# The crossed attentions of a two-layer block on one core: another order on all engines

## The reference, cut to what matters

```python
x = x + L0_xattn(layernorm(x), ctx, ...)
x = x + L0_ffn(layernorm(x), ...)            # routed experts and two shared ones
c = layernorm(x)                             # 2048 tokens
char2sub = softmax((c@Wq_c+bq_c) @ (ctx@Wk_s+bk_s).T / 16) @ (ctx@Wv_s+bv_s)
sub2char = softmax((ctx@Wq_s+bq_s) @ (c@Wk_c+bk_c).T / 16) @ (c@Wv_c+bv_c)
sub2char = interp_linear(sub2char, 2048)     # 1601 rows stretched to 2048
gate = sigmoid(concat(char2sub, sub2char) @ Wg + bg)
x = x + gate*char2sub + (1-gate)*sub2char
h = layernorm(x)
p = softmax(h @ gate_W.T);  cnt = sum(p > 0.3)
x = x + (experts 0 and 1 of h, each scaled by its count and its p) @ out_W.T
```

## Time and profile before

| | us |
|---|---|
| median of 3 runs | 1100.87 (1098.93 to 1103.83) |
| the profiled execution's own time | 1102.15 |
| its span, first to last instruction | 1100.3 |
| PE busy (share of the span) | 967.1 (88%) |
| DVE, ACT, POOL busy | 735.5, 588.6, 392.6 |
| mean granted clock of PE | 0.948 |

### The profile page before, as it was taken

The page is one execution under the profiler, slowest core; times in us unless marked ns, Lnnn a source line. Parts: engine busy times, 40 slices in busy tenths (PEclk is TensorE's granted clock), DMA queues, the critical chain, the costliest instruction groups (busy, mean ns, idle before and its releaser), DMA issues.

```text
span 1100.3 us, 19396 instructions
## 1 busy us (share of the span) xinstructions
PE 967.1 (88%) x6934; PEld 907.7 (82%) x6934; DVE 735.5 (67%) x1704; ACT 588.6 (53%) x1241; POOL 392.6 (36%) x607
## 2 busy tenths in 40 slices
PE   9999998999999999989889999999787687687575
PEld 8899996788999999878788989898787687687574
DVE  7677876686888888456656666656656646646654
ACT  6456665334777777433557556655544444445432
POOL 4424555172343432354000000001973544443451
PEclk9999999999999999999999999999988888888786
DMA  7200000214887886321200000001000000000000
GB/s 218 78 1 1 1 2 1 77 58 140 275 264 259 269 253 215 94 83 53 77 1 1 2 1 1 2 1 54 1 1 11 10 21 10 14 16 10 15 20 20
DMA packets 50950, 72.39 MB, mean 66 GB/s; under 512 B 5489, under 2 KB 33777, under 8 KB 50865
## 3 DMA queue, kind: packets, MB, share of 16 engines
q1 hardware_dynamic: 45152, 55.81, 16.3%
q0 software_dynamic: 5024, 14.42, 3.9%
q10 hardware_dynamic: 688, 1.05, 0.3%
HBM read 59.34 MB, written 11.93 MB: 65 GB/s over the span
## 4 chain that ended last, share of the span: by engine, by line
PE 29%; DVE 11%; ACT 5%; issue 3%; POOL 3%; ACTq 0%; DVEq 0%; POOLq 0%
PE wide L43 4%; PE wide L45 4%; PE wide L44 3%; PE wide L2108 3%; PE wide L2110 3%; PE wide L2109 3%; PE bank L43 2%; PE bank L44 2%; PE bank L45 2%; DVE Fx L2680 1%; PE bank L2132 1%; POOL CT_lo L2549 1%; DVE rows L2659 1%; ACT Fx L2330 1%; DVE X L2780 1%
## 5 line engine op out<-in xcount | busy, mean ns | idle before, releaser
L2108 PE MATMUL wide<-V_hi,pt 128*128 128x258 f32 x400 | 124.2, 310 | 16.0 <-DVE X L2707 7.0
L2110 PE MATMUL wide<-V_hi,pt 128*128 128x258 f32 x400 | 119.4, 299 | 0.0
L2109 PE MATMUL wide<-V_lo,pt 128*128 128x256 f32 x400 | 119.0, 298 | 0.0
L2108 PEld LDWEIGHTS wide<-V_hi,pt 128*128 128x128 f32 x400 | 83.0, 207 | 18.3 <-DVE pt L2685 17.5
L2547 POOL CAST CT_hi<-X 128x256 fp32r<-128x256 f32 x13 | 7.8, 600 | 226.1 <-PE bank L2110 226.0
L2659 DVE TENSOR_TENSOR rows<-rows,Fx 128x512 f32<-128x512 f32 (+2 forms) x63 | 40.6, 645 | 68.3 <-ACT Fx L2330 68.1
L2109 PEld LDWEIGHTS wide<-V_lo,pt 128*128 128x128 f32 x400 | 82.9, 207 | 0.2
L2110 PEld LDWEIGHTS wide<-V_hi,pt 128*128 128x128 f32 x400 | 82.6, 206 | 0.0
L2345 ACT ACTIVATE Fx<-Fx 128x512 f32<-128x512 f32 (+2 forms) x71 | 41.7, 587 | 67.1 <-DVE Fx L2680 67.1
L43 PE MATMUL bank<-rx_hi,expert_w_hi 128*128 128x256 f32 x256 | 73.5, 287 | 1.5 <-PEq L1100 1.5
L45 PE MATMUL bank<-rx_hi,expert_w_lo 128*128 128x256 f32 x256 | 71.5, 279 | 0.0
(11 more groups left out here) (519 smaller groups left out, 3677.5 us busy)
## 6 DMA issues: line engine op xcount, KB each, us to landing
sraw<-w1T SPq DMA_DIRECT2D x14, 512.0 KB, 5.1
sraw<-w3T SPq DMA_DIRECT2D x14, 512.0 KB, 6.1
sraw<-w2T SPq DMA_DIRECT2D x14, 512.0 KB, 7.0
raw_even<-w1T SPq DMA_DIRECT2D x11, 512.0 KB
raw_even<-w3T SPq DMA_DIRECT2D x11, 512.0 KB
raw_even<-w2T SPq DMA_DIRECT2D x11, 512.0 KB
routed_results<-rys POOLq DMA_DIRECT2D x15, 256.0 KB
X<-x SPq DMA_DIRECT2D x4, 512.0 KB, 6.4
```

The costliest lines, as they stand in the source:

```text
L2108: pe.matmul(dst[:, 0:D + 2], hi[:, x], v_hi(k), start=opens(n) and j == 0, stop=False)
L2109: pe.matmul(dst[:, 0:D], hi[:, x], v_lo(k), start=False, stop=False)
L2110: m = pe.matmul(dst[:, 0:D + 2], lo[:, x], v_hi(k), start=False, stop=closes(n) and k == keys_of(n)[-1])
```

## The change

It reorders the phase. The arithmetic stays, up to a few POOL instructions. In words: scores of groups 1 to 4 stand 13 blocks ahead (was 11), of groups 9 to 13 12 ahead (was 9), of groups 5 to 8 by lists; `subtract` goes up to five blocks ahead, `exponent` one step behind it; a group's blocks may be subtracted two steps after the maximum is turned. `weighted` sums tile by tile and counts `summed`, and `finish` of the first tile waits for that alone. The closing work of a token tile is dealt over more blocks; `x_turn` uses two banks in turn and asks for `out_done` one less. There are four token places. The context units stand in one list with their steps. Splitting the rows is four chunks, two high parts on ACT. Late weights are split at four successive steps. Cut to the core (`...` marks what is left out):

```diff
-            HEAD = 3
+            LEAD = 13
             behind = [[] for _ in range(NBLK)]
+            for m in range(first[1] + LEAD - first[1], first[SG - 1]):
+                behind[m - LEAD].append(m)
-            for b, at in enumerate([-3, -2, -1, -1, 0, 0, 1, 1, 1, 2, 2, 3, 3, 3, 4, 4]):
+            for b, at in enumerate([-5, -5, -4, -2, -2, -1, -1, 0, 0, 0, 1, 1, 1, 2, 2, 2]):
                 behind[first[SG - 2] + at].append(first[SG - 1] + b)
-            for b in range(7):
-                behind[first[SG - 1] + 5 + b].append(first[SG] + b)
-            for b, at in enumerate([-1, 0, 1, 1, 2, 3, 4]):
+            for b, at in enumerate([3, 4, 6, 7, 9, 10, 10]):
+                behind[first[SG - 1] + at].append(first[SG] + b)
+            for b, at in enumerate([-2, -1, 0, 1, 2, 2, 2]):
                 behind[first[SG] + at].append(first[SG + 1] + b)
             for g in range(SG + 2, NG):
                 for b in range(count[g]):
-                    behind[first[g - 1] + b - 2].append(first[g] + b)
+                    behind[first[g - 1] + b - (4 if g == SG + 2 else 5)].append(first[g] + b)
...
             def spread_step(g):
-                return -1 if g == 0 else max_step(g) + (0 if g > SG else 1)
+                return -1 if g == 0 else max_step(g) + 1
             def open_from(g):
-                return -1 if g == 0 else spread_step(g) + (1 if g >= SG else 0)
+                return -1 if g == 0 else spread_step(g) + 1
...
-            sub_end = [reached(n, 3) for n in range(-1, NBLK)]
-            high_end = [reached(n, 2) for n in range(-1, NBLK)]
+            sub_end = [reached(n, 5) for n in range(-1, NBLK)]
+            exp_end = [sub_end[0]] + sub_end[0:NBLK]
+            high_end = [min(reached(n, 2), e) for n, e in zip(range(-1, NBLK), exp_end)]
...
                 def token(i):
-                    o = (NC + i % 3) * D
-                    return X[:, o:o + D]
+                    o = (NC + i % 4) * D
+                    return X[:, o:o + D] if i % 4 < 3 else BV_C
+                ROW_CHUNKS = [(0, 2), (2, 6), (6, 10), (10, NC)]
...
                 def xb(i):
-                    return score_bank[1] if i == LAST else banks[1]
+                    return score_bank[1] if i == LAST else banks[1 + i % 2]
...
-                            pe.wait_ge(unit_low, 14)
+                            pe.wait_ge(unit_low, 6 if n < 6 else 16)
...
-                        for j, k in enumerate(keys_of(n)):
-                            for t in range(GROUPS[g][1]):
...
+                        for t in range(GROUPS[g][1]):
+                            if opens(n) and g:
+                                pe.wait_ge(finished, tiles_before[g - 1] + min(t + 1, GROUPS[g - 1][1]))
+                            dst = weighted_bank[t][0:chunk(g, t), :]
+                            for j, k in enumerate(keys_of(n)):
...
+                            if closes(n) and t + 1 < GROUPS[g][1]:
+                                m.then_inc(summed, 1)
...
-                        if 0 < i < LAST:
-                            pe.wait_ge(out_done, i)
+                        elif 1 < i < LAST:
+                            pe.wait_ge(out_done, i - 1)
...
+                    def closing_step(b, u, v):
+                        if b == 0 and real(u - 2):
+                            second_product(u - 2)
+                        if b == 1 and real(u):
+                            gate(u)
+                        if b == 2 and real(v - 2):
+                            x_turn(v - 2)
+                        if b == 2 and real(v):
+                            interpolate(v)
+                        if b == 3 and real(v - 2):
+                            first_products(v - 2)
+                        if b == 4 and real(v - 2):
+                            second_product(v - 2)
+                        if b == 4 and real(v):
+                            gate(v)
+                        if b == 5 and real(u):
+                            x_turn(u)
+                        if b == 5 and real(u + 2):
+                            interpolate(u + 2)
+                        if b == 6 and real(u):
+                            first_products(u)
...
                     for b in range(count[0]):
                         score(b)
...
-                    score(8)
+                    score(8)
+                    score(9)
                     max_turn(0)
-                    score(9)
+                    score(10)
                     spread_turn(0)
-                    score(10)
+                    score(11)
+                    fold(pe, wk, wq, bk, (banks[0], banks[1]), fold_low, 3, fold_done)
+                    score(12)
...
-                        dve.wait_ge(weighted_done, first[g + 1])
+                        if t + 1 < GROUPS[g][1]:
+                            dve.wait_ge(summed, tiles_before[g] - g + t + 1)
+                        else:
+                            dve.wait_ge(weighted_done, first[g + 1])
```

More of the change, by code:

```diff
@@ L2203, in _ @@
-                        if b == 5:
-                            interpolate(u + 2)
-                        for g in range(1, SG):
+                        if b == 3 and real(v):
+                            turn(v)
+                        for k in units_behind(n):
+                            later_unit(*k)
+                        for m in behind[n]:
+                            score(m)
+                        closing_step(b, u, v)
+                        for g in range(1, NG):
+                            if max_step(g) == n:
+                                max_turn(g)
@@ L2440, in _ @@
[L2440 to L2450 removed]
+                        middle_step(b, u, v)
@@ L2815, in _ @@
+                    late_weights = ((wa_hi, wa_lo, two(EW[:, 0, :])), (*ewb, two(EW[:, 1, :])), (g_hi, g_lo, rawg),
+                                    (rt_hi, rt_lo, two(rt_raw[:, :])))
                     for n in range(NBLK):
                         b, u, v = post(n)
+                        if closes(n):
+                            finish(group_of[n], 0)
+                        early_step(b, u, v)
+                        if closes(n):
+                            for t in range(1, GROUPS[group_of[n]][1]):
+                                finish(group_of[n], t)
+                        for m in behind[n - 1] if n else ():
+                            maximum(m)
@@ L2817, in _ @@
                         for m in range(sub_end[n], sub_end[n + 1]):
                             subtract(m)
[L2819 to L2824 removed]
                         for m in range(high_end[n], high_end[n + 1]):
                             low(m)
[L2827 removed]
+                        late_step(b, u, v)
@@ L2828, in _ @@
+                        for k in units_behind(n):
+                            later_unit(*k)
+                        if n == 7:
+                            folded_weight()
+                        for g in range(1, NG):
                             if max_step(g) == n:
                                 tops(g)
-                        if closes(n):
-                            for t in range(GROUPS[group_of[n]][1]):
-                                finish(group_of[n], t)
-                        if real(u - 1) and b == 0:
-                            x_split(u - 1)
@@ L2861, in _ @@
-                        for j in value_units_behind(n):
-                            value_unit(j)
-                        for m in behind[n]:
-                            maximum(m)
-                        if real(u) and b == 1:
-                            bias(u)
-                        if real(v) and b == 3:
-                            gate_low(v)
-                        if real(v) and b == 4:
-                            bias(v)
-                        if n < 2:
-                            fold_weight(n + 1)
```

631 lines of the change are left out of this document (318 added, 313 removed).

## The result

The kernel after takes 1010.17 us (median of four runs, 1008.3 to 1012.62) against 1099.9 for the kernel before in the same job (1097.31 to 1103.83): ratio 0.918, 95% interval 0.915 to 0.922. The forecast was 1000 us with a range of 978 to 1032, so the range held and the point was 10 us low. The profiled execution is the one of 1008.3 us, with a span of 1006.4 and a mean clock of 0.979.

What follows compares the result with a forecast made beforehand. PE was taken as the engine to feed, waiting for order, not capacity. Span 552.4 − 2 + 205 + 212.5 (groups 6 to 13) + 31 (tail) = 998.9, adjusted to 999.5, so 1000 us; range 978 to 1032.

Steps and rivals of the forecast that it cites:

- the signs set for being right: Token groups 27 to 30 us, clock over 0.95, PE's waits at the two transposes under 1, last group about 21.
- two set for being wrong: Among the signs of failure: DVE's maxima over 1 us near the row split, and a tail over 36 us.
- Part 1, lead-in: Ahead of the first score, key and value units moved: between 0 and 3 us gained, 2 taken.
- Part 2, groups 0 to 5: Context-row attention, scores 13 blocks ahead instead of 11: 205 us, a gain of 11.7; bounds 199 and 220.
- Full groups: Groups of two token tiles: 28.5 us each instead of 41.05, from PE's floor 26.5 and DVE at 27 or 28.
- Groups 6 and 7: First token groups: 26 us for group 6 (1.5 left for its end) and 27.5 for group 7.
- Groups 12 and 13: Last token groups: 24 us for group 12, bounded by DVE, and 21 for group 13, DVE 17 plus latency.
- Tail: After the last weighted sum: 31 us instead of 32.9, bounds 28 and 36, tile 14's gate starting no later.
- DVE's order as the bound: Rival, full groups: half of DVE's 15.9 us of waits stay, 33 us per group, 1025 us in all; chance 0.18.
- The rival of GpSimd's wide instructions: Wide POOL instructions block DVE: 8 us in group 6 and 1 a group after, 1014 us; chance 0.06.
- The lead is real: Rival denied here: places free late, evacuations wait, only the `out_done` wait goes, 1049 us; chance 0.04.
- lockstep: Rival: PE and DVE overlap nothing, a group takes 51.7 us, 1160 us in all; chance 0.03.

Runs made afterwards that it cites:

- The bank experiment: Kernel before with only the closing products' bank alternating between two and `out_done` asked for one tile earlier: 1087.59 us, ratio 0.989.
- the lead experiment: Kernel after with the scores of groups 9 to 13 ten blocks ahead instead of twelve: 1033.25 us, ratio 0.940.
- the best kernel: Kernel after with row split in pieces, PE's tail reordered, odd tile's turn behind the score, late weights two steps later: 992.53 us, ratio 0.903.
- the experiment with added work: Kernel after with one idle 512-element DVE reduction ahead of each low part from group 8 on: 1027.68 us, ratio 0.936.

## Why the prediction was right, and where its sizes were off

**The mechanism was right.** PE was waiting for order, not capacity: the waits at the two transposes fell from 67.2 us to 11.1, the clock in a full group rose to 1.00, and the groups are 28.4 long. The bank experiment (12 us) and the lead experiment (23) show two parts of it; the rest of the 90 is not divided by any run. Of the signs set for being right one was missed by little, the odd tile's turn waits 1.2 us and not under 1, and two set for being wrong did show: DVE's maxima over 1 us near the row split and a tail over 36.

**Part 1, lead-in.** 2 us forecast, 4.9 in the two profiled executions. With starts that scatter over 4.8 us in kernels whose code is the same up to there, one execution can't size this term; the two executions with the old order stand at 552.37 and 553.60, the middle of the twelve with the new one near 549.3, so 3 to 4.

**Part 2, groups 0 to 5.** 205 us forecast, 198.75 measured, just under the low bound of 199. The 8.5 us that I left for idle time and clock were too much: PE idles 198.75 − 196.95 = 1.8 us and the clock is 0.99. The wait of 2.57 us at the first weighted sum went entirely: the fold's products and two more score blocks now stand ahead of it and cover the chain that I priced at 3. With part 1, group 6 begins 9.2 us before its forecast time.

**Full groups.** 28.5 forecast, 28.4 measured in groups 9 to 11, by a sum that was wrong in both terms. DVE did not grow to 27 or 28 us beside GpSimd: it is busy 24.93, against 24.53 before. PE's floor was not 26.5 but 27.20 busy, and 1.20 us of waiting for the turned tile makes 28.4. My walk through the queues had ACT's maximum spreading 1 us late at that point and let PE's score cover it; the code had the turn ahead of the score. With the turn behind it the period is about 27.5: from the start of group 8 to the wait at L2137 in group 12 the best kernel takes 119.56 us, its like without that edit (row split and weights) 123.24, 0.9 less in each of the four. There PE is busy for all of group 9, 27.49 of 27.49 us:

```profile
831.11:858.60 27.49, 27.49 (x230) 27.07 (x229) 24.91 (x63) 18.22 (x47) 15.79 (x20) 1.00 0.07 21
```

**Groups 6 and 7.** 26 and 27.5 forecast, 31.6 and 31.0 measured: 9.1 us over. This is the step that failed. The sentence was "Late weights are spread over four steps: the same DVE and ACT work", and the row split "in sum it takes no more than before". Both count work and not what it holds up. Cutting up the one and moving the other took 5.4 us off group 6 (31.65 to 26.25), of the 5.6 that it was over the forecast. Of the end of group 6 I had reserved 1.5 us and it takes 4.0. The 3.5 us over in group 7 are a wait of 1.32 us at its end and a clock of 0.91 behind the gap; the best kernel still needs 29.9 there (774.24 to 804.16).

**Groups 12 and 13.** 24 and 21 forecast, 26.0 and 20.2 measured. In group 12 DVE is busy 23.14 us where I had 22.2 and 2 of waits; no run takes it further apart.

**Tail.** 31 forecast with 28 and 36 as bounds, 38.6 measured: outside. The sentence that failed is "tile 14's gate starts no later". I priced the tail by what is left to do and not by the order in which PE's queue has it: the products of tile 13 stand ahead of the gate of tile 15 and wait for a split. In the better order the tail is the 31 that I had written, 30.8. The clock falls with it: 0.72 over the tail.

The deviations add up: −9.2 (start of group 6), +5.6, +3.5, −1.2 (four full groups), +2.0, −0.8, +7.6 = +7.5, and 998.9 + 7.5 = 1006.4, the measured span. The point was near since two errors of 9 us met: the self-contained part came out better than its bound, and the seams (where one kind of group passes into the next, and the end) worse. That the point came within 10 us is in part luck.

**The range.** The low bounds as the prediction lists them take 22 to 24 us off 1000, which gives 976 to 978 and not 973. So the range began at them and not 5 us over; the result was far from that end.

**The rivals.** DVE's order as the bound (0.18, 1025 us) was not the outcome: DVE's work in a full group hides behind PE. But the margin is thin, 0.8 us in a full group by the experiment with added work and not the 3 that the prediction had. The rival of GpSimd's wide instructions (0.06, 1014 us) was right that they hold DVE up in group 6, where a maximum took 2.29 us and a low part 2.88, and wrong in its price: cutting them up gave 0.7 us of group 6 by itself, 5.4 with the late weights moved and not 8, and in a full group DVE's busy time rose by 0.4 us (24.53 to 24.93), not 1. The lead is real (cutting it costs 23 us), and lockstep did not occur.

## What to carry to other kernels

Price a rewritten order at its seams, not only in the steady state: here the steady group came out at the forecast and everything that was off lay in the first groups of a kind and in the tail, where a waiting instruction stood in front of ones that were ready. On an engine with an order of its own, put the instruction whose input comes last behind those that can run; three such moves, none of which takes away work, gave 17.6 us together with a finer split. Where two loads hold up one chain, each edit alone may show nothing (1.5 us of 6.3): try them together before dropping either.

## What the runs showed of the hardware

The same DVE subtraction took four times as long beside a wide GpSimd subtraction. The timeline of DVE and GpSimd in group 6 of the kernel after:

```profile
751.22 2.41 POOL L2590 TENSOR_TENSOR CT_lo<-X,CT_hi 128x1024 fp32r<-128x1024 f32 x1 [1.75 <-ACT CT_hi L2483]
751.63 2.54 DVE L2722 TENSOR_TENSOR pt<-Fx,pt 128x512 fp32r<-128x512 f32 x1 [0.44 <-ACT pt L2364]
...
755.22 2.66 POOL L2590 TENSOR_TENSOR CT_lo<-X,CT_hi 128x1024 fp32r<-128x1024 f32 x1
755.54 2.88 DVE L2722 TENSOR_TENSOR pt<-Fx,pt 128x512 fp32r<-128x512 f32 x1
...
759.58 2.29 DVE L2696 TENSOR_TENSOR rows<-rows,Fx 128x512 f32<-128x512 f32 x1
```

The DVE instruction that starts 0.3 us after the GpSimd one ends 0.5 us after it; alone it takes some 0.68. With GpSimd's pieces at 256 columns the longest such DVE instruction in this stretch is 1.23 us. By the Trainium skill ("SBUF — State Buffer", SBUF: two separate sides, and Who interferes with whom) a DVE instruction with two SBUF inputs takes its second one through the read port that it shares with GpSimd, and the port pair is an exclusive lock that is held for a whole instruction; the trace agrees, 2.88 us beside 2.66. I had seen only holds of 0.2 us before and gave the case 0.06. In these two kernels the longest hold goes with the length of one GpSimd instruction, and GpSimd's total is no guide: in pieces it is busy longer, 24.83 us instead of 18.76 in group 6, and DVE 4.5 us less.
